# Attention and two mixture-of-experts layers on one core: projection steps moved, and the two experts found by two rounds of a maximum

## What is computed

```python
xn = _layernorm(x, axis=-1)
x = x + attention(xn) + moe(xn)
```

```python
# layer 0
scores = xf @ W_gate + b_gate
topk_val, topk_idx = jax.lax.top_k(scores, TOP_K)
h = jax.nn.relu(jnp.einsum('nd,edh->neh', xf, W1) + b1)
y = jnp.einsum('neh,ehd->ned', h, W2) + b2      # weighted by topk_val
# layer 1
gates = jax.nn.softmax(x_flat @ Wg + bg, axis=-1)
topk_gates, topk_idx = jax.lax.top_k(gates, K)
topk_gates = topk_gates / jnp.sum(topk_gates, axis=1, keepdims=True)
expert_out = jnp.einsum('nd,edo->neo', x_flat, We) + be
```

## Time and profile before

| | before |
|---|---|
| median of 3 runs | 3185.12 us |
| the profiled execution's own time | 3198.38 us |
| its span, first to last instruction | 3196.6 us |
| mean granted TensorE clock | 0.982 of 2.4 GHz |
| PE busy | 3013.7 us (94% of the span) |
| DVE busy | 2392.2 us (75%) |
| ACT busy | 1981.2 us (62%) |
| POOL busy | 1024.4 us (32%) |

### The profile page before, as it was taken

One profiled execution on the slowest core, in us unless ns is written; L12 is line 12 of the kernel. 1 busy time (PEld: TensorE's weight loads), 2 busy tenths in 40 slices (PEclk: granted clock), 3 DMA queues, 4 the chain that ended last, 5 costly groups with the idle time before them and its releaser, 6 DMA issues.

```text
span 3196.6 us, 62083 instructions
## 1 busy us (share of the span) xinstructions
PE 3013.7 (94%) x19056; PEld 1579.7 (49%) x19056; DVE 2392.2 (75%) x7245; ACT 1981.2 (62%) x4954; POOL 1024.4 (32%) x1244
## 2 busy tenths in 40 slices
PE   5799999999999999999999999999999999999998
PEld 3454544445455554544545555454545555445443
DVE  5676768777786777878777787777877767687784
ACT  2466656666666666666666666666666666666665
POOL 4115134151432413334151331513324142241512
PEclk7899999999999999999999999999999999999999
DMA  6767455363554535446374563635546365453642
GB/s 188 201 169 209 133 157 152 107 195 110 180 184 145 184 122 176 133 130 188 100 216 139 167 182 120 190 97 166 161 132 209 120 192 153 145 156 103 185 135 77
DMA packets 328103, 496.03 MB, mean 155 GB/s; under 512 B 56832, under 2 KB 242656, under 8 KB 327776
## 3 DMA queue, kind: packets, MB, share of 16 engines
q1 hardware_dynamic: 293536, 416.99, 43.7%
q0 software_dynamic: 24576, 67.14, 6.9%
q10 hardware_dynamic: 9664, 7.93, 0.9%
HBM read 344.19 MB, written 152.84 MB: 155 GB/s over the span
## 4 chain that ended last, share of the span: by engine, by line
PE 79%; DVE 10%; issue 4%; ACT 3%; DMA 2%; SPq 1%; POOL 1%; another core or an unknown queue 0%; DVEq 0%; ACTq 0%; POOLq 0%
PE po L1144 16%; PE pmx L1094 15%; PE pst L1081 14%; PE pst L1128 9%; PE pmx L1214 5%; PE pst L1113 5%; PE pst L1225 4%; PE pmx L1183 4%; PE pst L1102 3%; DVE pmx L843 3%; DVE x L975 2%; PE pmx L1162 2%; PE pst L1150 1%; ACT probs L686 1%; DMA xg<-x_slots 1%
## 5 line engine op out<-in xcount | busy, mean ns | idle before, releaser
L686 ACT ACTIVATE probs<-pst 128x512 f32<-128x512 f32 (+3 forms) x3072 | 1402.8, 496 | 450.9 <-PE pst L1081 422.9
L595 POOL TENSOR_SCALAR_AFFINE_SELECT probs<-probs 128x512 f32<-128x512 f32 x512 | 332.5, 650 | 1686.3 <-ACT probs L686 1684.7
L839 DVE TENSOR_REDUCE rmax<-pmx 128x1 f32<-128x512 f32 x1024 | 668.9, 683 | 142.4 <-PE pmx L1094 134.5
L1081 PE MATMUL pst<-qs,k_first 98*128 98x512 bf16 (+3 forms) x2048 | 693.8, 344 | 34.3 <-ACT xgT L691 17.6
L843 DVE CUSTOM_DVE_ANT_0 pmx<-pmx,mask,rmax 128x128 f32<-128x128 f32 (+3 forms) x1024 | 537.5, 556 | 217.2 <-PE pmx L1094 189.0
L1094 PE MATMUL pmx<-k_first,qs 96*128 96x512 bf16 (+2 forms) x2048 | 672.6, 346 | 28.0 <-issue 9.3
L1144 PE MATMUL po<-probs,v 128*32 128x512 f32 (+3 forms) x6144 | 663.5, 504 | 14.6 <-POOL probs L595 10.6
L843 DVE CUSTOM_DVE_ANT_0 pmx<-pmx,mask 128x128 f32<-128x128 f32 (+3 forms) x1024 | 482.8, 510 | 168.1 <-PE pmx L1094 152.8
L1094 PEld LDWEIGHTS pmx<-k_first,qs 96*128 96x128 bf16 x2048 | 199.8, 99 | 377.8 <-issue 172.1
L1094 PE MATMUL pmx<-k_second,qs 96*128 96x128 bf16 (+3 forms) x1024 | 305.9, 303 | 28.3 <-DVE otok L955 14.5
L1081 PE MATMUL pst<-qs,k_second 98*128 98x512 bf16 (+3 forms) x1024 | 302.4, 302 | 5.8 <-issue 3.8
(11 more groups left out here) (121 smaller groups left out, 3379.9 us busy)
## 6 DMA issues: line engine op xcount, KB each, us to landing
wt<-w_tiles SPq DMA_DIRECT2D x161, 513.0 KB
qk_parts<-parts SPq DMA_DIRECT2D x256, 192.0 KB
xg<-x_slots SPq DMA_DIRECT2D x368, 128.0 KB
y_slots<-ys SPq DMA_DIRECT2D x368, 128.0 KB
wt<-w_tiles SPq DMA_DIRECT2D x184, 256.0 KB
qs<-qk_parts SPq DMA_DIRECT2D x128, 192.0 KB
qs<-qk_parts SPq DMA_DIRECT2D x128, 128.0 KB
k_first<-qk_parts SPq DMA_DIRECT2D x64, 192.0 KB, 2.9
```

The source lines that it names most:

```text
L595: pool.affine_select(out=tri, in_=tri, compare_op=ALU.is_ge, fill=0.0, base=0, pattern=[[0, GH], [1, P]], channel_multiplier=-1).then_inc( ...
L686: act.activation(probs[:, u % 2, j, 0:w], ps[:, 0:w], ACT.Exp, scale=DH ** -0.5).then_inc(st_read, 1)
L839: dve.tensor_reduce(rmax0[:, col:col + 1], src, AX_X, ALU.max).then_inc(mx_read, 1)
L1081: pe.matmul(ps[:, 0:w], keys[0:SROWS, j, k % HT * P:(k % HT + 1) * P], qs[0:SROWS, set_no(q, n) % QRING, j, a:a + w], start=True, stop=Tru ...
```

## The change

- `PROJ`: the eight projections move from places 22, 24, 30, 32, 38, 40, 46, 0 to 15, 17, 23, 25, 35, 37, 3, 7. With them move everything that hangs on a projection's step, and `store_parts`: from places 26, 34, 42 and 2 to 19, 27, 39 and 9.
- `LOAD_Q` moves from places 29, 33, 37, 41 (first half) to 22, 25, 38, 42, and `LOAD_K` from 31, 35, 39, 45 to 21, 28, 40, 44. The loads of the second half stay.
- The choice of the experts: parts 6 to 10 take the maximum of the 8 values, find the first expert that has it by a countdown 8, 7, ... 1, lower that expert's value, and do the same again. `chosen` (two rows of 8) and `best` (two values) take the place of the rank. Parts 12, 13, 21, 25 and 26 follow from them; the old part 26 (a sum for `gpick`) is gone.
- POOL makes the constant `countdown` at the start.

```diff
-GATE_PLACES = [0, 2, 3] + list(range(8, 21)) + list(range(24, 36))
+GATE_PLACES = [0, 2, 3] + list(range(8, 21)) + list(range(24, 35))
...
-PROJ = {(0, 0): -26, (0, 1): -24, (0, 2): -18, (0, 3): -16, (1, 0): -10, (1, 1): -8, (1, 2): -2, (1, 3): 0}
-LOAD_Q = (-19, -15, -11, -7, 1, 5, 13, 19)
-LOAD_K = (-17, -13, -9, -3, -1, 9, 16, 25)
+PROJ = {(0, 0): -33, (0, 1): -31, (0, 2): -25, (0, 3): -23, (1, 0): -13, (1, 1): -11, (1, 2): 3, (1, 3): 7}
+LOAD_Q = (-26, -23, -10, -6, 1, 5, 13, 19)
+LOAD_K = (-27, -20, -8, -4, -1, 9, 16, 25)
...
                 elif part == 6:
-                    dve.tensor_tensor(cgt[:], other, own, ALU.is_gt)
+                    link(dve.tensor_reduce(best[:, :, 0], value, AX_X, ALU.max))
+                    link(dve.tensor_tensor(equal[:], value, best[:, :, 0:1].broadcast_to([P, NT, E]), ALU.is_equal))
                 elif part == 7:
-                    link(dve.tensor_tensor(cge[:], other, own, ALU.is_ge))
+                    link(dve.tensor_tensor(equal[:], equal[:], countdown[:], ALU.mult))
+                    link(dve.tensor_reduce(gtot[:], equal[:], AX_X, ALU.max))
                 elif part == 8:
-                    link(dve.tensor_tensor(cge[:], cge[:], earlier[:].unsqueeze(1).broadcast_to([P, NT, E, E]),
-                                           ALU.mult))
+                    link(dve.tensor_tensor(chosen[:, :, 0], countdown[:], tile_e(gtot), ALU.is_equal))
+                    link(dve.scalar_tensor_tensor(out=others[:], in0=chosen[:, :, 0], scalar=LOWEST, in1=value,
+                                                  op0=ALU.mult, op1=ALU.add))
                 elif part == 9:
-                    link(dve.tensor_tensor(cgt[:], cgt[:], cge[:], ALU.max))
+                    link(dve.tensor_reduce(best[:, :, 1], others[:], AX_X, ALU.max))
+                    link(dve.tensor_tensor(equal[:], others[:], best[:, :, 1:2].broadcast_to([P, NT, E]), ALU.is_equal))
                 elif part == 10:
-                    link(dve.tensor_reduce(rank[:], cgt[:], AX_X, ALU.add))
+                    link(dve.tensor_tensor(equal[:], equal[:], countdown[:], ALU.mult))
+                    link(dve.tensor_reduce(gtot[:], equal[:], AX_X, ALU.max))
                 elif part == 11:
-                    dve.tensor_scalar(picks[:], rank[:], 1.5, None, ALU.is_lt).then_inc(picks_ready, 1)
+                    link(dve.tensor_tensor(chosen[:, :, 1], countdown[:], tile_e(gtot), ALU.is_equal))
+                    dve.tensor_tensor(picks[:], chosen[:, :, 0], chosen[:, :, 1], ALU.add).then_inc(picks_ready, 1)
                 elif part == 12:
-                    pick = dve.scalar_tensor_tensor(out=picked, in0=rank[:], scalar=1.5, in1=value,
-                                                    op0=ALU.is_lt, op1=ALU.mult)
                     if l == 1:
-                        link(pick)
-                        link(dve.tensor_reduce(gtot[:], picked, AX_X, ALU.add))
-                    else:
-                        pick.then_inc(gate_ready, 1)
-                elif part == 13 and l == 1:
-                    link(dve.reciprocal(ginv[:], gtot[:]))
-                    dve.tensor_tensor(picked, picked, tile_e(ginv), ALU.mult).then_inc(gate_ready, 1)
+                        link(dve.tensor_tensor(gtot[:], best[:, :, 0], best[:, :, 1], ALU.add))
+                        link(dve.reciprocal(ginv[:], gtot[:]))
+                        link(dve.tensor_tensor(best[:], best[:], ginv[:].unsqueeze(2).broadcast_to([P, NT, 2]), ALU.mult))
+                    for k in range(2):
+                        ins = dve.tensor_tensor(gsel[:, :, k], chosen[:, :, k],
+                                                best[:, :, k:k + 1].broadcast_to([P, NT, E]), ALU.mult)
+                    link(ins)
+                elif part == 13:
+                    dve.tensor_tensor(picked, gsel[:, :, 0], gsel[:, :, 1], ALU.add).then_inc(gate_ready, 1)
...
                 elif part == 21:
-                    for k in range(2):
-                        ins = dve.scalar_tensor_tensor(out=sel[:, :, k], in0=rank[:], scalar=float(k), in1=pos[:],
-                                                       op0=ALU.is_equal, op1=ALU.mult)
-                    link(ins)
+                    link(dve.tensor_tensor(sel[:], chosen[:], pos[:].unsqueeze(2).broadcast_to([P, NT, 2, E]), ALU.mult))
...
                 elif part == 25:
-                    dve.wait_ge(gate_ready, q + 1)
-                    for k in range(2):
-                        ins = dve.scalar_tensor_tensor(out=gsel[:, :, k], in0=rank[:], scalar=float(k), in1=picked,
-                                                       op0=ALU.is_equal, op1=ALU.mult)
-                    link(ins)
+                    dve.tensor_copy(gpick[:, q % 2], best[:].rearrange("p t k -> p (t k)"))
                 elif part == 26:
-                    link(dve.tensor_reduce(gpick[:, q % 2], gsel[:].rearrange("p t k e -> p (t k) e"), AX_X, ALU.add))
-                elif part == 27:
                     dve.tensor_scalar(expert[:, q % 2, 0:NTILE], tsum[:], -1.0, None, ALU.add).then_inc(experts_ready, 1)
```

More of the change, by code:

```diff
@@ L277, in attention_moe_kernel @@
         ginv = sb("ginv", [P, NT])
-        rank = graw
         gate = sb("gate", [P, NT, GR])
@@ L281, in attention_moe_kernel @@
         gparts = sb("gparts", [P, NT, 6, GR], BF16)
-        cgt = sb("cgt", [P, NT, E, E])
-        cge = sb("cge", [P, NT, E, E])
+        best = sb("best", [P, NT, 2])
+        equal = sb("equal", [P, NT, E])
+        others = sb("others", [P, NT, E])
+        chosen = sb("chosen", [P, NT, 2, E])
+        countdown = sb("countdown", [P, NT, E])
         earlier = sb("earlier", [P, E, E])
@@ L644, in _ @@
                       allow_small_or_imprecise_dtypes=True)
+            pool.iota(countdown[:], pattern=[[0, NT], [-1, E]], base=E, channel_multiplier=0,
+                      allow_small_or_imprecise_dtypes=True)
             link(pool.memset(gate[:, :, E:E + 1], 1.0))
@@ L852, in gates @@
                 rows = lambda a: a[:, :, 0:E + 1]
-                other = value.unsqueeze(2).broadcast_to([P, NT, E, E])
-                own = value.unsqueeze(3).broadcast_to([P, NT, E, E])
                 if part == 0:
```

## The result

The changed kernel takes 3230.34 us, median of four runs (3226.06 to 3238.29), against 3187.24 us before (also four runs, one more than ahead of the prediction): a ratio of 1.0136, interval 1.0112 to 1.016. The forecast was 3118 us with a range of 3085 to 3165: wrong in sign. The profiled execution took 3229.5 us (span 3227.8), so it stands for the median.

The account below looks back on a forecast made before the run. The sum of PE's work was taken to bound the kernel, so only time in which PE is held up could be regained. Terms -32 - 36 + 3 - 2 = -67 us took 3185.1 to 3118 us, range 3085 to 3165.

Parts of the forecast that it names:

- The experts' choice: -32 us: Steps 25 to 27: shorter DVE chain and moved projections end step 26's wait for DVE, 2.13 us a run, 32 us.
- The stores: -36 us: Steps 35 and 36: stores and loads leave the scattered rows' queue, so the joint stop goes, 2.43 us a run.
- Three engines that stop and resume together wait for one thing outside them: Steps 35 and 36: reading of ACT and DVE resuming together at 2013.6 after 2.2 us without work, PE stopped too.
- rival 2: Steps 35 and 36: stores did not freeze the queue; 8 instead of 36 us gained, 3146 us; chance 0.13.
- so nothing behind it waits: SP's queue, steps 19 and 20: a store takes 2.9 us to issue in 9.7 us, so tile tokens and weights don't wait.
- Projections that move out of cover: +3: Steps 46 and 0 to 3 and 7: step 7 costs 1.8 us, mostly given back; +0.2 a run, +3 us.
- The start: -2: First tiles: the store ahead of the buffer clearing goes, some 3 us; step 7's projection costs up to 1.8 us.
- Rival 5: Steps 9, 27 and 39: the freeze travels with the stores, 109 us come against 67, 3227 us; chance 0.08.
- The clock: Step 26 and steps 35 and 36: granted clock 0.78 and 0.84 in the stalls, to return to 1.00 at both.

Follow-up runs that it names:

- e1: Changed kernel with projections, stores and loads back at the places of before, so only the new choice of experts is new: 3173.7 us, ratio 0.9952.
- e2: Kernel before with the new places of projections, stores and loads; the choice by comparisons stays: 3234.9 us, ratio 1.0134.
- e5: e1 with POOL starting scattered row n only when row n-2 has landed: 3223.8 us, ratio 1.0098.
- e11: e1 with two pauses: POOL waits before rows 4 and 8 until all earlier rows have landed: 3197.7 us, ratio 1.0026.
- e3: Changed kernel with the store of step 39 issued one step later, behind the first tile's weights: 3202.6 us, ratio 1.0039.
- e6: Changed kernel with the second half's projections, their stores and the loads for sets 2 and 3 back at the places of before: 3164.2 us, ratio 0.9908.
- run 15: Not a follow-up kernel: a numbered pass through the steps inside one profiled execution, after the fifteen whole runs 0 to 14; no time of its own given.
- e4: Changed kernel with at most two scattered rows under way: 3208.3 us, ratio 1.0057.
- e7: e6 with at most two scattered rows under way: 3159.4 us, ratio 0.9887.
- run 9: Not a follow-up kernel: a numbered pass through the steps in the profiled execution before the change; PE's signal counts stand still from 2010.6 to 2013.6.
- e8: e3 with at most two scattered rows under way: 3192.2 us, ratio 0.9997.
- e10: e6 with two pauses: POOL waits before rows 4 and 8 until all earlier rows have landed: 3156.3 us, ratio 0.9899.
- e12: e6 with one pause: POOL waits before row 6 until all earlier rows have landed: 3182.2 us, ratio 0.9982.

## Why the prediction was wrong, point by point

By the places of the terms, runs 0 to 14 of the two profiled executions differ by -27.9 us in steps 15 to 33 (forecast: -32 for the choice), by -2.9 in 34 to 41 (-36 for the stores), by +43.7 in 42 (nothing) and by +18.1 in 43 to 47 and 0 to 14 (+3).

- **"The experts' choice: -32 us": right in place and size.** The forecast of 2.13 us a run is 25.6 in twelve. Step 26 lost 28.4 us by its rows, and steps 15 to 33 together, which also hold what came back in steps 27, 28, 31 and 33, lost 21.9. DVE's own part (1.2 a run) was measured in e1, where step 26 is 1.25 shorter. The other half, put down to the moved projections, fits the 28.2 of both together, but e2 shows that the moves alone take 23.2 there: the two parts overlap and can't be split as the working did. The Trainium skill (VectorE: DVE Perf Modes, "The TRN2 errata") gave 0.8 us by its formula; the rows' 1.2 was the better estimate. Most of the new small instructions take 0.21 to 0.23 us in the changed kernel, which agrees with the 0.22 that the page's formula gives for 64 values. The executions that take 0.4 to 1.2 us (11 of the 16 of L877 among them) all lie beside POOL's subtraction of a low part. The same explains the 0.98 of the earlier trace rows, which the working took as one duration: of the 16 executions of L880 before, five take 0.69 us, and the eleven beside such a subtraction 0.99 to 1.23.
- **"The stores: -36 us": the step that failed first.** Steps 35 and 36 are rid of their stop as forecast (-30.4 us in twelve runs against 29.1), but the cause was misread, and the stop came back in step 34 for +30.1. "Three engines that stop and resume together wait for one thing outside them" was the false premise: the earlier trace rows gives PE as what released ACT and DVE, and POOL's rows wait for PE by the program. The reading of the earlier trace rows named everything that was in flight there, and picked the stores because they were large and would go. e5 and e11 keep them and have no stop. What decides, as far as the edits tell, is POOL's rows at equal distances in the same timeline, and the change takes out what had opened gaps in that string (`low_parts` in steps 31 and 33). The text did say that `low_parts` leaves the scattered steps and took it for relief. This term should have been near 0 (over the fifteen whole runs steps 34 to 41 together gave 2.9 us), and rival 2 (0.13) held the right thought: rows and tiles suffice. Its evidence, a share of 0.93 without a stop in the earlier trace rows, was weightier than it was given: the gathered rows there go in pairs, with POOL idle for 1.1 us or more between the pairs of run 12, so that place holds no string.
- **Step 42: not in the sum, +38.2 us in twelve runs, 43.7 in the fifteen from 0 to 14.** The sentence "so nothing behind it waits" was worked out for the store of steps 19 and 20, and only for it. The same question for the store of step 39 was never put: behind it on SP's queue stand the first tile's weights, wanted three steps on. And of the projections moved from 38 and 40 to 35 and 37 only their own price was counted, not that they had been the time between the last row and the first tile. e3 prices the order (28 us by the medians), e6, which undoes both and with them the loads of sets 2 and 3, shows that together they are the whole of it.
- **"Projections that move out of cover: +3": under-sized.** Step 7 cost 1.71 us a run as said (1.8); steps 0 to 5 gave back 9.2 us in twelve runs, less than assumed. All of steps 43 to 47 and 0 to 14 is +10.9 us in twelve runs, 18.1 in runs 0 to 14, inside the bounds of -15 to +27. Most of it is step 7, +20.6 in twelve.
- **"The start: -2": right.** At step 8 of the first run the changed kernel is 1.8 us ahead. (What lies before run 3 and from run 15 on is together 1.6 us longer, since it holds three periods with the new stalls.)
- **Rival 5 gave 3227 us, and the time was 3230, but this is a coincidence.** It wanted a joint stop with the stores in steps 9, 27 and 39. Steps 9 and 10 went from 84.4 to 86.9 us in twelve runs and step 27 from 47.8 to 50.0, with no such stop. The store that cost much, that of step 39, did so through the order of SP's queue.
- **The clock** came back to 1.00 in step 26, as said, and fell anew where the new stalls are.

Step 42's cause is shown by edits (e3, e6). That the stop needs no stores is shown by the changed kernel and e6, and that it goes when POOL's rows are held apart, with stores beside them or without, by e4, e5 and e7. Not settled is how the rows hold up PE's products or their signals, and whether their number under way or their distance matters.

## What to carry to other kernels

When a transfer or a step is moved, write down for each instruction that it is put ahead of, on each queue, who waits for it and by when, and do it for every one of the moved transfers and not for the first. Work that goes away from between a producer and its consumer was cover: count it as a loss there, even if its own time is the same elsewhere. And when several things are in flight at an unexplained stop, don't credit the change with removing it because it removes one of them; an edit that removes only that one costs one run and would have shown it. A pace on a queue that works in order is paid for by all that stands behind it (here the mask).

## What the runs showed of the hardware that was not expected

- POOL issues scattered rows (an indirect transfer of 128 rows) every 1.27 us when nothing holds it (0.96 us for the issue, 0.30 between). Near the end of a string PE, ACT and DVE stop together for 1 to 3 us. The others wait for PE, whose signals stand still for 3.0 us in run 9 before, though its products are listed. A limit of two rows under way removes it (e4, e5, e7, e8). Groups of four with a wait for their landing between leave a shorter form, 7.7 us in twelve runs of e10. Six in a row bring it (after, e12), and so do four after a gap (before, three runs of e12). It doesn't hang on the traffic alone: the rows that hold it show 129 GB/s and 36% (after), 88 GB/s and 24% (e12) and 299 GB/s and 90%. How the rows reach PE no view shows, and it stays open.
- A stall of a few us can cost more than itself: the granted clock lay between PE's two levels (1.2 and 2.4 GHz) in the rows of long ones shown above, 0.83, 0.81 and 0.68, against 1.00 in the same step where the stall was gone (e4 in step 34, run 3). In run 3 of the changed kernel it was 1.00 inside the stop and 0.50 for 3.4 us behind it, when PE was busy again.
- DVE instructions that read two operands in SBUF took 0.4 to 1.2 us instead of 0.2, and 0.99 to 1.23 instead of 0.69, where POOL subtracted a low part (`parts<-rest,parts`) beside them (the new small ones, and L880 before).
